# A two-chain recurrent kernel with its second chain moved half a round behind the first

## What is computed

```python
h = relu(layernorm(x))                      # x: (16, 512, 128)
h = relu(adj @ (h @ Wg0 + bg0))             # adj: (512, 512), per batch
h = relu(adj @ (h @ Wg1 + bg1))
for p in 1, 2, 3, 4:                        # an LSTM per p over windows of p tokens
    nw = 512 // p
    last = lstm_last(Wih[p-1], Whh[p-1], b[p-1], windows(h, p))   # p steps, zero start
    h[:, p-1 :: p] = last                   # last hidden state to each window's last token
x = x + h
h = relu(layernorm(x))
agg = A_hat @ h                             # A_hat: normalised adj + I
z  = agg @ W1.T + b1                        # 256 features
z2 = relu(batchnorm(z)) @ W2.T + b2         # batchnorm over all 16 * 512 rows
x  = x + batchnorm(z2)
```

## Time and profile before

| what | us |
|---|---|
| median of 3 runs | 639.04 |
| the profiled execution | 635.4 |
| its span, first to last instruction | 633.5 |
| first turn starts | 69.8 |
| rounds 0, 1, 2, 3 | 123.3, 124.6, 124.8, 96.6 |
| last h to batch norm (tail) | 30.5 |
| batch norm to the span's end | 63.9 |
| TensorE, VectorE, ScalarE, GpSimd busy | 529.4, 448.2, 329.7, 203.7 |

### The profile page before, as it was taken

How to read it: one execution, slowest core, us unless ns; L and a number is a source line. 1 busy time by engine, 2 the same in 40 slices (tenths; PEclk the granted TensorE clock), 3 DMA queues, 4 the chain that set the end, 5 groups by cost and what they waited for, 6 DMA issues and landing times.

```text
span 633.5 us, 9027 instructions
## 1 busy us (share of the span) xinstructions
PE 529.4 (84%) x2769; PEld 452.0 (71%) x2769; DVE 448.2 (71%) x1033; ACT 329.7 (52%) x620; POOL 203.7 (32%) x308
## 2 busy tenths in 40 slices
PE   3679869988997699999958999999599989675656
PEld 3468748877995588989846899889377878454436
DVE  3454367888875688878566887884777887756776
ACT  3423535454555365555554656566456556245554
POOL 2340263202004652222054531310640220609952
PEclk9769979989799799999997999999899999796998
DMA  7210000100000201101021011010011101792007
GB/s 216 67 35 1 1 5 30 66 18 1 17 2 24 77 1 68 51 2 52 1 101 66 0 67 50 1 50 33 34 51 50 51 1 51 273 401 89 1 1 265
DMA packets 20075, 37.45 MB, mean 59 GB/s; under 512 B 1690, under 2 KB 6212, under 8 KB 20036
## 3 DMA queue, kind: packets, MB, share of 16 engines
q1 hardware_dynamic: 19332, 36.60, 16.2%
q10 hardware_dynamic: 704, 0.39, 0.2%
HBM read 22.30 MB, written 14.68 MB: 58 GB/s over the span
## 4 chain that ended last, share of the span: by engine, by line
issue 42%; PE 23%; POOL 16%; DVE 9%; POOLq 5%; ACT 4%; DMA 1%; DVEq 1%; ACTq 0%; SPq 0%
POOL z_back L391 4%; POOLq L321 3%; POOL y_post L323 3%; PE gate_ps L977 3%; PE gate_ps L979 3%; PE gate_ps L978 3%; POOL x_pre L323 3%; PE pre_ps L977 2%; PE pre_ps L978 2%; PE pre_ps L979 2%; POOL h L346 2%; PE post_ps L977 1%; PE post_ps L979 1%; PE post_ps L978 1%; POOLq L319 1%
## 5 line engine op out<-in xcount | busy, mean ns | idle before, releaser
L580 ACT ACTIVATE gate<-gate_ps,gate_bias 128x256 f32<-128x256 f32 (+2 forms) x312 | 163.8, 565 | 52.9 <-PE gate_ps L979 31.2
L977 PE MATMUL gate_ps<-by_class_hi,wih_hi 128*128 128x256 f32 (+2 forms) x264 | 88.8, 336 | 20.2 <-DVE by_class_lo L663 16.0
L596 ACT ACTIVATE gate<-cell 128x512 f32<-128x512 f32 (+2 forms) x88 | 45.2, 514 | 99.5 <-DVE cell L841 60.0
L978 PE MATMUL gate_ps<-by_class_hi,wih_lo 128*128 128x256 f32 (+2 forms) x264 | 87.0, 330 | 0.0
L979 PE MATMUL gate_ps<-by_class_lo,wih_hi 128*128 128x256 f32 (+2 forms) x264 | 86.9, 329 | 0.0
L977 PEld LDWEIGHTS gate_ps<-by_class_hi,wih_hi 128*128 128x128 f32 x264 | 52.5, 199 | 26.8 <-issue 15.0
L351 POOL TENSOR_TENSOR cell<-gate 128x512 f32<-128x512 f32 x16 | 20.6, 1288 | 147.7 <-ACT gate L580 142.9
L977 PE MATMUL gate_ps<-hstep_hi,whh_hi 128*128 128x256 f32 (+2 forms) x192 | 60.7, 316 | 0.0
L979 PE MATMUL gate_ps<-hstep_lo,whh_hi 128*128 128x256 f32 (+2 forms) x192 | 60.6, 316 | 0.0
L978 PE MATMUL gate_ps<-hstep_hi,whh_lo 128*128 128x256 f32 (+2 forms) x192 | 60.6, 315 | 0.0
L978 PEld LDWEIGHTS gate_ps<-by_class_hi,wih_lo 128*128 128x128 f32 x264 | 52.6, 199 | 4.2
(11 more groups left out here) (244 smaller groups left out, 1429.2 us busy)
## 6 DMA issues: line engine op xcount, KB each, us to landing
z_spill<-z_ring SPq DMA_DIRECT2D x12, 512.0 KB, 2.9
z_back<-z_spill SPq DMA_DIRECT2D x12, 512.0 KB, 9.3
x_pre<-in_x SPq DMA_DIRECT2D x16, 256.0 KB, 2.8
x<-in_x SPq DMA_DIRECT2D x16, 256.0 KB, 3.0
x_spill<-x SPq DMA_DIRECT2D x16, 256.0 KB, 2.0
x_back<-x_spill SPq DMA_DIRECT2D x1, 4096.0 KB, 22.8
out<-x_back SPq DMA_DIRECT2D x16, 256.0 KB, 2.4
x<-in_adj SPq DMA_DIRECT2D x1, 1024.0 KB, 5.9
```

The lines of the kernel that those rows point to most:

```text
L580: nc.scalar.activation(gate[:, chain, g, 0:size], gate_ps[k % GATE_BANKS][:, 0:size], ACT.Tanh if g == G_GATE else ACT.Sigmoid, bias=gate_ ...
L596: nc.scalar.activation(gate[:, chain, G_GATE, 0:size], cell[:, chain, 0:size], ACT.Tanh)\
L977: nc.tensor.matmul(ps, w[0], m[0], start=start, stop=False)
L978: nc.tensor.matmul(ps, w[1], m[0], start=False, stop=False)
```

## The change

Chain 1 runs half a round (11 slots) behind chain 0. Time is cut into nine halves of 11 slots (`HALF`, `HALVES_RUN`, `N_SLOTS`). In an even slot position of a half one chain, 0 in even halves and 1 in odd ones, does its steps 0 to 5 (p = 1 twice, p = 2 twice, p = 3's first two); in an odd position the other chain does its steps 6 to 10 (p = 3's last, p = 4's four). So half 0 has six turns of chain 0 alone, and half 8 five turns of chain 1 alone.

- Input and output units sit at fixed positions of a half, for two batches a half: `PRE_POS` and `POST_POS`, first the even batch, then the odd one (a position below 0 is in the half before). The prologue does the input work of two batches instead of four. Output work runs in halves 2 to 8, and the tail has two batches instead of four.
- All rounds are written out; there is no loop. Waits are on constants.
- On ScalarE a p = 1 turn is like any other: gates, then tanh. Only its G gate waits, for the previous h and even tokens. On GpSimd cell and even tokens of a turn follow each other (`first_turn`). VectorE writes the p = 1 h over the cell instead of the I gate.
- z of batches 8 to 11 stay in `z_ring` and those of 12 to 15 go straight to `z_back`, so only eight z are spilled and read back; their reads are issued in half 7. x1 of the last four batches stays in `x1`.
- `turn` always uses `post_ps`. The degree steps are at slots 1, 2, 3 and 5, the hat chunks at 8, 10, 12 and 14.
- The order of tensors in memory changes, so that `z_back` lies on what half 7 no longer uses.

```diff
-TURNS = [(chain, *step) for step in STEPS for chain in range(CHAINS)]
+LEAD = 6
+HALF = len(STEPS)
+HALVES_RUN = CHAINS * ROUNDS + 1
+N_SLOTS = HALF * HALVES_RUN
+def step_in(slot):
+    half, pos = divmod(slot, HALF)
+    if pos % 2 == 0:
+        chain, r, s = half % 2, half // 2, pos // 2
+    else:
+        chain, r, s = (half + 1) % 2, (half - 1) // 2, LEAD + pos // 2
+    return (r, chain, s) if 0 <= r < ROUNDS else None
...
-PRE_TURN = {"stats": (1, 4, 7, 13), "norm": (3, 6, 10, 16),
-            AGG0: (4, 9, 13, 18), LIN0: (5, 10, 14, 19), LIN1: (6, 11, 15, 20), AGG1: (7, 12, 17, 21)}
-POST_TURN = {"turn": [T_AT[b] for b in range(PER_ROUND)], "agg": (4, 8, 14, 19), "hid0": (6, 9, 16, 20),
-             "hid1": (7, 10, 17, 21), "norm": (3, 6, 12, 17), "stats": (1, 4, 9, 15)}
-DEG_SUM, DEG_TOKENS, DEG_POW, DINV_DIAG, DINV_ROWS = 3, 3, 4, 5, 7
-HAT_CHUNK = (8, 11, 14, 17)
+EARLY = SUBS
+PRE_POS = {"stats": (-4, 3), "norm": (-2, 5), AGG0: (0, 6), LIN0: (1, 7), LIN1: (2, 8), AGG1: (3, 10)}
+POST_POS = {"turn": (0, 1), "agg": (5, 8), "hid0": (6, 9), "hid1": (7, 10), "norm": (4, 7), "stats": (2, 4)}
+IN_PROLOGUE = [(kind, EARLY + i) for kind, spots in PRE_POS.items() for i in range(SUBS) if spots[i] < 0]
+PRE_AFTER = [[(kind, n) for kind, spots in PRE_POS.items() for n in range(EARLY, BATCHES)
+              if HALF * (n // SUBS - 1) + spots[n % SUBS] == slot] for slot in range(N_SLOTS)]
+POST_AFTER = [[(kind, n) for kind, spots in POST_POS.items() for n in range(BATCHES - SUBS)
+               if HALF * (n // SUBS + 2) + spots[n % SUBS] == slot] for slot in range(N_SLOTS)]
+DEG_SUM, DEG_TOKENS, DEG_POW, DINV_DIAG, DINV_ROWS = 1, 1, 2, 3, 5
+HAT_CHUNK = (8, 10, 12, 14)
...
+            def first_turn(g):
+                r, chain, p, step, sub, nb = TURNS[g]
+                pool.wait_ge(gates_act, GATES_BEFORE[g] + 2)
+                if sub > 0:
+                    pool.wait_ge(class_lo, CLASS_AT[r, chain, 1, sub - 1])
+                nc.gpsimd.tensor_tensor(cell[:, chain, :], gate[:, chain, I_GATE, :],
+                                        gate[:, chain, G_GATE, :], ALU.mult).then_inc(first_cell, 1)
+                pool.wait_ge(tanh_ready, g + 1)
+                if r > 0:
+                    pool.wait_ge(turn_mm, batch_of(r - 1, chain, sub) + 1)
+                nc.gpsimd.tensor_tensor(h32[:, chain, 0::2, sub], gate[:, chain, O_GATE, 0:T // 2],
+                                        gate[:, chain, G_GATE, 0:T // 2], ALU.mult).then_inc(even_done, 1)
...
+            for half in range(HALVES_RUN):
+                m, n = SUBS * (half + 1), SUBS * (half - 2)
...
+                if m == BATCHES:
+                    sp.wait_ge(pre_lo, 4 * BATCHES)
+                    for b in range(SPILLED):
+                        if b < PER_ROUND:
+                            sp.wait_ge(z_out[b], 16 * (SPILLED // PER_ROUND))
+                        sp.dma_start(z_back[:, b, :], z_dram[b]).then_inc(z_in[b], 16)
+                if 0 <= n < LATE:
+                    store_x1(n)
+                    store_x1(n + 1)
+                    load_x1(n + 4)
...
+            for slot, g in enumerate(TURN_AT):
+                if g is not None:
+                    lstm_turn(g)
+                deg_steps(slot)
+                for kind, n in PRE_AFTER[slot]:
+                    if kind in SPLITS:
+                        pre_unit(kind, n, pre_ps, 0)
+                for kind, n in POST_AFTER[slot]:
+                    if kind == "turn":
+                        if n == 0:
+                            pe.wait_ge(hat_part, 5 * CHUNKS)
+                        elif n % SUBS == 0:
+                            pe.wait_ge(z_ready, 2 * n)
+                        else:
+                            pe.wait_ge(x1_ready, n)
+                        turn(n, post_ps)
```

More of the change, by code:

```diff
@@ L111, in later @@
-def later(r, more):
-    return not isinstance(r, int) or r > 0 or more > 0
-def class_count(chain, p, step):
-    return CLASS_AT[(chain, 1, SUBS - 1) if p == 2 else (chain, p, step)]
-def g_count(r, b):
-    return 8 * (b // 2) + 7 + b % 2 if isinstance(r, int) and r == 0 else at(r, N_PRE, 4 * b + 4)
+EARLY = SUBS
+PRE_POS = {"stats": (-4, 3), "norm": (-2, 5), AGG0: (0, 6), LIN0: (1, 7), LIN1: (2, 8), AGG1: (3, 10)}
+POST_POS = {"turn": (0, 1), "agg": (5, 8), "hid0": (6, 9), "hid1": (7, 10), "norm": (4, 7), "stats": (2, 4)}
@@ L265, in build, with pre_number, z_new, z_end @@
                                                             ("bank", CHUNKS + 1), ("norm", 0), ("norm", 1)])
[L266 to L281 removed]
+        for _k in range(4):
+            PROLOGUE += [(_k, 0), (_k, 1)]
+            if _k in (AGG0, LIN1):
+                PROLOGUE += [(kind, n) for kind, n in IN_PROLOGUE if kind == ("stats" if _k == AGG0 else "norm")]
+            PROLOGUE += [("bank", 6 + 2 * _k), ("bank", 7 + 2 * _k)]
+        assert PROLOGUE[-1] == ("bank", len(BANKS) - 1)
+        def pre_number(n, k):
+            return 2 * k + n if n < EARLY else 4 * n + k
+        def z_new(n):
+            return z_ring[:, n % PER_ROUND, :] if n < LATE else z_back[:, n - PER_ROUND, :]
+        def z_end(n):
+            return z_back[:, n, :] if n < SPILLED else z_new(n)
+        def x1_end(n):
+            return x1_back[:, n, :] if n < LATE else x1[:, n % PER_ROUND, :]
         def pre_parts(k, b, ps, i):
@@ new lines, in _ @@
+            for slot, g in enumerate(TURN_AT):
+                if g is not None and TURNS[g][2] == 1:
+                    first_turn(g)
+                for kind, n in PRE_AFTER[slot]:
+                    if kind == "stats":
+                        norm_pre(n)
+                for kind, n in POST_AFTER[slot]:
+                    if kind == "stats":
+                        norm_post(n, y_post)
+                if slot == DEG_POW:
+                    pool.wait_ge(deg_ready, 1)
+                    nc.gpsimd.tensor_tensor(dinv[:, :], deg[:, :], minus_half[:, :], ALU.pow).then_inc(dinv_ready, 1)
@@ L378, in batch_norm @@
+            for n in range(BATCHES - SUBS, BATCHES):
+                norm_post(n, y_last[n % 2])
             def batch_norm(bn, var, rstd):
@@ L628, in _ @@
+            last = range(BATCHES - SUBS, BATCHES)
+            for n in last:
+                normed(n, y_last[n % 2][:, :], nrm[n % 2], post_y, post_nhi)
+            for n in last:
+                agg_out(n, gate_ps[n % 2], n % 2)
+            for n in last:
                 for half in range(HALVES):
-                    hid_out(rho, b, half, gate_ps[2 + (2 * b + half) % 4], True)
+                    hid_out(n, half, gate_ps[2 + 2 * (n % 2) + half])
             for k, b in enumerate(END_ORDER):
@@ L916, in _ @@
+            last = range(BATCHES - SUBS, BATCHES)
+            for n in last:
+                turned(n, (pre_ps, post_ps)[n % 2])
+                stats_post(n)
+            for n in last:
+                normed(n, y_last[n % 2][:, :], nrm[n % 2], post_nhi, post_nlo)
+            for n in last:
+                agg_out(n, gate_ps[n % 2], n % 2)
+            for n in last:
                 for half in range(HALVES):
-                    hid_stats(rho, b, half)
+                    hid_stats(n, half)
@@ new lines, in _ @@
+            last_two = range(BATCHES - SUBS, BATCHES)
+            for n in last_two:
+                if n % 2 == 0:
+                    pe.wait_ge(pre_lo, 4 * BATCHES)
+                else:
+                    pe.wait_ge(z_ready, 2 * (BATCHES - SUBS))
+                turn(n, (pre_ps, post_ps)[n % 2])
+            pe.wait_ge(gates_act, N_GATES)
+            for n in last_two:
+                agg_mms(n, gate_ps[n % 2], n % 2)
+            for n in last_two:
+                pe.wait_ge(agg_lo, n + 1)
```

691 lines of the change are left out of this document (283 added, 408 removed).

## The result

The changed kernel takes **658.38 us** (median of 4 runs, 657.07 to 658.81); the kernel before took 638.9 beside it (638.19 to 639.62). The ratio is 1.030, with a 95% interval of 1.0283 to 1.032: slower, and above the range of 612 to 651. The profiled execution took 658.19, its span 656.3.

What follows compares the result with a forecast made beforehand. TensorE, 84% busy, was taken as the bound behind a bad start of each round. 54.0 + 55 + 55 + 297.5 + 48.5 + 33 + 20 + 63.9 = 626.9 us of span, so 632 us, 1.1% faster; range 612 to 651.

Steps and rivals of the forecast that it cites:

- the waits of the halves at both ends: Halves 0, 1, 7 and 8, waits included, were forecast at 55, 55, 48.5 and 33 us.
- the walk of the steady half: Halves 2 to 6: TensorE's 54.9 us plus 5.7 of waits gave 60.6 each; 59.5 was taken.
- The upper bound, 62.3: Halves 2 to 6: the most a steady half should take, 62.3 us, the old pace.
- until 19.7: Half 0: TensorE, followed slot by slot from 0, waits for u_lo until 19.7 us, ahead of AGG1.
- the 2.7 that I had added for slow matmuls: Half 0: 2.7 us for slow matmuls behind a wait, added to 52.3 to give 55.
- In half 8 the walk: Half 8, chain 1 only: TensorE's turns and waits followed to the last h at 34; 33 us taken, bounds 28 and 38.
- I priced the tail from the intervals of before: Tail: two batches instead of four, 8.3 us less and about 2 more off; 20 us, bounds 18 and 24.
- VectorE becomes the bound: Rival, chance 0.27: VectorE's in-order queue sets the pace, halves 62.3 us, total 649, slower.
- The waits fill: Rival, chance 0.20: in steady halves slack hides both TensorE waits, a half 56.5 us, total 617.
- The clock falls in halves 0, 1 and 8: Rival, chance 0.08: some 16 us of TensorE work there at half clock, +8 us, total 640.
- The h of a p = 1 turn: VectorE's h beside GpSimd kept at 1.36 us; at 0.67 the sum would be 3.5 us less.
- the first turn: Prologue: batches 2 and 3 leave it (-17.6 us), weight banks add 1.8; first turn at 54.0 instead of 69.8.

Runs made afterwards that it cites:

- Experiment 1: Changed kernel with AGG1 (input-side adjacency product) of the even batch at slot 4 of a half instead of 3: 648.07 us, ratio 1.0148.
- experiment 8: Changed kernel with the even batch's AGG1 at slot 4 and the odd input batch's statistics moved to slot 9 of the half before: 640.98 us, ratio 1.0079.
- experiment 4: Changed kernel with 49 matmuls that nobody reads put ahead of the long waits of halves 7 and 8: 656.76 us, ratio 1.0293.
- experiment 10: Changed kernel with batch 13's adjacency product and both hidden products moved behind the last turn of half 8: 657.45 us, ratio 1.03.
- experiment 12: Kernel of experiment 9 with transposes, residual adds and statistics of batches 14 and 15 directly behind the last h: 629.28 us, ratio 0.9884.
- experiment 3: Changed kernel with the statistics of z over 64 of 512 tokens, so its result differs: 654.67 us, ratio 1.0271.
- experiment 9: Kernel of experiment 8 with the output units one slot later as well: 631.47 us, ratio 0.9915.
- experiment 5: Changed kernel with the eight z reads issued after the rounds instead of in half 7: 657.2 us, ratio 1.0344.

## Why the prediction was wrong

Two steps failed: the waits of the halves at both ends were summed too short, and the walk of the steady half was discounted. They are 18.5 and 10.0 of the 29.4 us; each alone is more than the 6.6 us of span by which I had the kernel faster.

**The steady halves, +10.0.** My walk gave 60.6 us, and I took 59.5 because I thought its stamps too coarse. The measured half is 61.4: TensorE is busy 56.4 where I summed 54.9, and the waits are 2.31 + 1.92 + 0.70 = 4.93 where I summed 5.7. Undiscounted the walk was 0.8 us off, discounted 1.9. Five times 1.9 is 9.5 of the 10.0 in the table. With the walk as it stood the forecast would have been 632.4 us of span for 633.5 before: no gain worth the name, but still 24 short of the 656.3. The walk also had the places right (u_lo ahead of AGG1, nrm_lo ahead of `agg`), which experiments 1 and 8 confirm by moving them. The upper bound, 62.3, held but for half 2 (62.8), where matmuls at half clock stand behind the wait for u_lo; I had no half clock in the steady halves.

**The halves at both ends, +18.5 us in halves 0, 1, 7 and 8.** In half 0 the wait for u_lo was in the walk, "until 19.7", and ended at 19.4. The walk slid behind it, counted from 52.7: p = 2's second step at 30.9 (29.6 predicted), that step and AGG0 over at 40.8 (37.8), a wait of 1.41 for agg_lo that the walk hasn't, p = 3's second step at 49.3 (45.9), its first 18 matmuls at half clock, AGG1 over at 58.2 (52.3, and 55 with the 2.7 that I had added for slow matmuls). In half 1 I summed VectorE's work and its waits without a walk at all; the waits of 3.71 and 4.15, each with slow matmuls behind it, stand in it unnamed. Experiment 1 took the u_lo waits out, put waits only 0.6 us shorter in their place, and gained 10 us here: 6.0 of idle time, the rest mostly fewer matmuls at half clock. Half 7 has the same kind of waits, 2.96 for by_class_lo and 3.05 for nrm_lo, at a clock of 0.90. In half 8 the walk slid as follows, counted from 530.8: p = 4 at 9.7 (8.4 predicted), its second step 14.4 (13.0) and over at 19.7 (15.8), since its 24 matmuls took 5.3 us at half clock and not 2.8; third step 25.0 (21.1); product of batch 13 at 31.9 (27.0); last h 39 (34). Half clock is the first slip, but not the larger part: experiment 4 held the clock at 1.00 up to 561 and won 3.2 us at the third step, of which 0.4 was left at the last h. What stood ahead of the last step cost more: with the product of batch 13 behind it (experiment 10) the last h came 4.2 us sooner.

**In-order queues at the end, +2.3 in the tail.** I priced the tail from the intervals of before and not unit by unit. In the changed kernel the last transposes start at 571.18, 1.0 us behind the end of the last h, so little stands ahead of them; but the 24 products of the last two batches, behind 6.95 us of idle time, take 8.0 us (579.78 to 587.82) where they are 5.5 at full clock, and the sum had no term for that. In the tail of before the product behind a wait of 3.69 (547.19) started slow too and is in the intervals that I used, so how much of the 2.3 it is stays open. Experiments 10 and 12 show that the product of batch 13 holds up the last turn by 4.2 us, and that the same units, put behind it, hold up the tail.

**The rivals.** "VectorE becomes the bound" gave 649 and the right sign, by a mechanism that experiments 3 and 8 rule out: it is the time of single results in VectorE's queue, not its sum. "The waits fill" was wrong in the halves as they were placed; with the positions moved as in experiment 9 they filled to 59.7, not to 56.5. "The clock falls in halves 0, 1 and 8" happened (0.89, 0.92, 0.87, and 0.90 in half 7), with an effect that I can't split cleanly from the waits that let it fall.

**The h of a p = 1 turn**, priced at 1.36 us: in the changed kernel it takes 0.69 (minimum 0.684, median 0.692, maximum 1.231 of 16). VectorE and GpSimd in a steady half:

```profile
310.26 0.69 DVE L856 TENSOR_TENSOR cell<-gate 128x512 f32<-128x512 f32 x1 [1.74 <-ACT gate L600]
310.30 1.24 POOL L365 TENSOR_TENSOR h<-gate 128x256 f32<-128x256 f32 x1 [0.74 <-ACT gate L600]
310.98 0.84 DVE L858 CAST by_class_hi<-cell 128x512 fp32r<-128x512 f32 x1
```

VectorE starts 0.04 us ahead of GpSimd and runs unhindered; the cast behind it, which meets GpSimd under way, takes 0.84 instead of 0.43. In the earlier trace rows GpSimd's cell (200.54 to 201.83) was under way when h began at 201.02: I had called that starting together, and it was not. The one slow h of the 16, 1.23 us at 115.49, began 0.18 us behind GpSimd's operation. The rule of the Trainium skill ("SBUF — State Buffer", "SBUF: two separate sides"), whoever starts first has the port pair for a whole instruction, agrees with both traces, and the prediction should have priced the step by it. It is worth 0.67 us here (h to lo takes 2.29, 310.26 to 312.55, for 2.96; the cast's 0.84 was in the 2.96 already), most of why the wait ahead of AGG1 is 2.31 and not 3.2.

**What held**: the first turn (52.7 for 54.0), the end (63.8), the z reads at nothing that shows (experiment 5), and TensorE's work of a steady half within 3%.

**What stays open.** How much of halves 0 and 1 is clock and how much wait; nothing was run that holds the clock there. Why the clock fell behind the wait of 2.33 us in half 2, and not behind the same wait in the halves after it, isn't known either.
